# The up projection of a language adapter wholly in rounded parts, with new orders of a step

## The chip, the core and the metric

The program runs on one core of a Trainium2 chip. The metric is the device time of one execution in microseconds (us). TensorE (PE) multiplies matrices, VectorE (DVE), ScalarE (ACT) and GpSimd (POOL) work on elements, and SyncE (SP) issues DMAs. A queue that issues a DMA is written with a q (SPq, ACTq).

## What is computed

There are 32 samples of 512 tokens with 512 features, all in float32. Each sample has its own adapter (one of 10 languages) and its own linear layer (one of 32 categories):

```python
# per sample: w1 = W1[lang], w2 = W2[lang], ... , W = L1_W[cat]
h = relu(x @ w1 + b1)                     # 512x512 @ 512x128, the up projection
r = x + (h @ w2 + b2)                     # 512x128 @ 128x512, the down projection
normed = (r - mean) * rsqrt(var + 1e-5)
x1 = x + (normed * gamma + beta)
out = x1 + (x1 @ W + b)                   # 512x512 @ 512x512, the linear layer
```

## The kernel before, in words

**Precision.** A float32 factor is split into a rounded part `_hi` and the rest `_lo` (type fp32r), and a product is taken as three matmuls, hi x hi, lo x hi and hi x lo (`split_product`, L833 to L835). One float32 matmul does the same without any split, and PE spends more time on it. The identity is added to W ahead of the linear layer, so that x1 @ (W + 1) gives x1 + x1 @ W.

**Stages.** The kernel is written by hand for each engine, as a software pipeline with one `step(k)` per sample. In step k PE does the linear layer of sample k-2, the up and down projections of sample k, and the transposes of the normalised sample k-1. Its order is: linear tiles 0 and 1 (`linear_tile`, 12 matmuls each), `up(k)`, `turn_norm` 0 and 1, linear tile 2, `down(k)`, `turn_norm` 2 and 3, linear tile 3. A linear tile sums over four chunks c of the features. In tile 0 each chunk waits for its own part of the data: `w_lo` from POOL and `x1T_lo` from DVE (L902, L903). So tile 0 of step k+1 waits for what DVE's `low_x1` wrote in step k, chunk by chunk.

**Up projection.** It has four chunks too. Three (NS = 3) are done from rounded parts `xs_hi`, `xs_lo`, `w1_hi`, `w1_lo`, nine matmuls. The fourth is one float32 matmul (L876), which the trace records as two instructions. ACT makes the `_hi` parts of the next sample (`high_xs_of_next`, `high_w1_of_next`), POOL the `_lo` parts (`low_xs`, `low_w1`).

**The chain inside a step.** After `up(k)` ACT does `relu` (two instructions), and DVE takes the rest (`low_h`). PE runs `down(k)`. DVE adds the result to x (`y_pair`, L680) and takes the means, ACT squares each of four token tiles (`square`, L537) and takes a root (`deviation`, L542), and DVE finishes the inverse deviation in seven small instructions (`variance`, `inverse_deviation`, L699 to L716). ACT normalises in the next step (L501), PE transposes, DVE forms x1 (`x1`, L725), ACT rounds it (`high_x1`, L518) and DVE takes the rest (`low_x1`, L731). Both `x1` halves of a step (chunks 0 and 1, then 2 and 3) are for sample k-1.

**Buffers and queues.** Every engine runs its instructions in the order in which they are written. SP issues nearly all DMAs in one order per step; ACT issues two of the four `x_quad` loads, which DVE then transposes into `xT` (L666). `params` (gamma, beta, b1 of a language) and `b2_bc` have two buffers each. Stores leave by halves: `out_half0` holds tiles 0 and 1, `out_half1` tiles 2 and 3.

## Time and profile before

| what | value |
|---|---|
| median of 3 runs | 614.54 us (614.09 to 615.64) |
| the profiled execution's own time | 615.36 us |
| its span in the profile | 613.5 us |
| PE busy | 605.9 us, 99% of the span |
| DVE, ACT, POOL busy | 520.5 (85%), 514.2 (84%), 525.7 us (86%) |
| HBM traffic | 270 GB/s over the span |

The span runs from the first to the last instruction in the trace, and the execution's own time is 1.86 us longer. Busy is the sum of an engine's instruction times. A group of instructions also has a mean duration and the idle time of its engine ahead of it. The share of PE in the chain of work that ended last is 86%.

### The profile page before, as it was taken

The page shows a single profiled execution, that of the slowest core. Times are in us where ns is not written, and L with a number is a line of the kernel's source. Part 1 is how long each engine was busy: PE and PEld are TensorE (multiplying, and loading weights), DVE is VectorE, ACT ScalarE, POOL GpSimd, SP SyncE. Part 2 cuts the span into 40 slices and gives each one's busy share as a digit, 9 for nine tenths or more (in the row PEclk, how much of TensorE's full clock was granted, in tenths as well). Part 3 has the DMA queues.
Part 4 walks back from the last instruction along what each step waited for, and adds up shares of the span by engine and source line. Part 5 has one row for each costly group of instructions (what it writes and reads, how often), then busy time and mean ns, then how long its engine had stood idle before and what let it go on. Part 6 is the DMA issues. An engine that isn't in the chain of part 4 may idle for free.

```text
span 613.5 us, 10721 instructions
## 1 busy us (share of the span) xinstructions
PE 605.9 (99%) x2866; PEld 490.3 (80%) x2866; DVE 520.5 (85%) x1151; ACT 514.2 (84%) x772; POOL 525.7 (86%) x265
## 2 busy tenths in 40 slices
PE   9998999999999999999999999999999999999998
PEld 7766888778888888888888888778888888888887
DVE  1889889789898888988989899898898888899673
ACT  4978888789888899888889889889888989889770
POOL 5789998799989999888998889899888998989830
PEclk9999999999999999999999999999999999999999
DMA  9987899878998888899898997989999898997422
GB/s 305 236 273 247 299 317 286 268 257 264 309 301 272 285 284 274 300 289 301 252 303 255 311 295 257 296 265 289 309 289 291 261 296 263 314 308 269 160 87 104
DMA packets 125939, 166.24 MB, mean 271 GB/s; under 512 B 11062, under 2 KB 72768, under 8 KB 121812
## 3 DMA queue, kind: packets, MB, share of 16 engines
q1 hardware_dynamic: 94900, 150.12, 75.0%
q10 hardware_dynamic: 30912, 15.73, 9.2%
q8 instruction: 11, 0.18, 0.1%
q14 instruction: 20, 0.16, 0.1%
q0 software_dynamic: 96, 0.05, 0.0%
HBM read 132.17 MB, written 33.55 MB: 270 GB/s over the span
## 4 chain that ended last, share of the span: by engine, by line
PE 86%; DMA 4%; SPq 3%; DVE 3%; ACT 2%; issue 2%; POOL 0%; ACTq 0%; DVEq 0%; POOLq 0%
PE o_bank L833 17%; PE o_bank L835 17%; PE o_bank L834 17%; PE n_bank L851 8%; PE d_bank L833 5%; PE d_bank L835 5%; PE d_bank L834 5%; PE d_bank L876 4%; DMA x_quad<-in_x 2%; PE y_bank L833 2%; PE y_bank L835 2%; PE y_bank L834 2%; DMA x_tok<-in_x 2%; SPq L243 1%; DVE xT L666 1%
## 5 line engine op out<-in xcount | busy, mean ns | idle before, releaser
L833 PE MATMUL o_bank<-w_hi,x1T_hi 128*128 128x512 f32 x512 | 205.4, 401 | 1.8 <-DVE x1T_lo L731 1.8
L835 PE MATMUL o_bank<-w_hi,x1T_lo 128*128 128x512 f32 x512 | 200.0, 391 | 0.0
L834 PE MATMUL o_bank<-w_lo,x1T_hi 128*128 128x512 f32 x512 | 199.1, 389 | 0.0
L666 DVE STREAM_TRANSPOSE xT<-x_quad 128x512 f32<-128x512 f32 x120 | 127.2, 1102 | 38.7 <-DMA x_quad<-in_x 38.7
L428 POOL TENSOR_TENSOR w_lo<-w_raw,w_hi 128x1024 fp32r<-128x1024 f32 x62 | 149.3, 2408 | 10.5 <-ACT w_hi L511 10.4
L501 ACT ACTIVATE norm<-y,neg_mean_rstd,rstd 128x512 f32<-128x512 f32 x128 | 151.8, 1262 | 1.1 <-DVE neg_mean_rstd L716 1.1
L423 POOL TENSOR_TENSOR x_tok<-x_tok,b_bc 128x1024 f32<-128x1024 f32 x60 | 145.0, 2417 | 4.5 <-issue 2.6
L518 ACT ACTIVATE x1T_hi<-n_bank,params 128x512 fp32r<-128x512 f32 x126 | 85.2, 690 | 35.3 <-DVE n_bank L725 26.9
L833 PEld LDWEIGHTS o_bank<-w_hi,x1T_hi 128*128 128x128 f32 x512 | 96.3, 188 | 21.7 <-issue 3.8
L835 PEld LDWEIGHTS o_bank<-w_hi,x1T_lo 128*128 128x128 f32 x512 | 96.1, 188 | 21.0
L834 PEld LDWEIGHTS o_bank<-w_lo,x1T_hi 128*128 128x128 f32 x512 | 96.4, 188 | 17.8
L537 ACT ACTIVATE x_tok<-y,neg_mean 128x512 f32<-128x512 f32 x128 | 91.9, 719 | 17.7 <-DVE neg_mean L686 17.7
L394 POOL TENSOR_TENSOR xs_lo<-xT,xs_hi 128x1536 fp32r<-128x1536 f32 x29 | 102.3, 3527 | 0.0
L725 DVE SCALAR_TENSOR_TENSOR n_bank<-n_bank,params,xT 128x512 f32<-128x512 f32 x126 | 92.4, 757 | 7.1 <-PE n_bank L851 6.8
L731 DVE SCALAR_TENSOR_TENSOR x1T_lo<-n_bank,params,x1T_hi 128x512 fp32r<-128x512 f32 x126 | 91.1, 750 | 7.4 <-ACT x1T_hi L518 2.0
L743 DVE TENSOR_TENSOR out_half<-o_bank,b_bc 128x512 f32<-128x512 f32 x127 | 85.5, 673 | 12.4 <-PE o_bank L835 11.6
L511 ACT ACTIVATE w_hi<-w_raw 128x1024 fp32r<-128x1024 f32 x64 | 67.6, 1059 | 17.4 <-POOL w_raw L405 16.1
L382 POOL TENSOR_TENSOR w_lo<-w_raw,w_hi 128x512 fp32r<-128x512 f32 x31 | 40.4, 1304 | 44.1 <-ACT w_hi L486 42.0
L851 PEld LDWEIGHTS n_bank<-ident,norm 128*128 128x128 f32 x504 | 59.2, 145 | 9.4 <-ACT norm L501 2.4
L851 PE MATMUL n_bank<-ident,norm 128*128 128x128 f32 x504 | 65.9, 274 | 0.1
L405 POOL TENSOR_TENSOR w_raw<-w_raw,ident 128x512 f32<-128x512 f32 x32 | 50.4, 1575 | 0.0
L833 PE MATMUL d_bank<-xs_hi,w_hi 128*128 128x512 f32 x87 | 46.0, 529 | 0.0
(95 smaller groups left out, 818.0 us busy)
## 6 DMA issues: line engine op xcount, KB each, us to landing
w_raw<-in_L_cond_W SPq DMA_DIRECT2D x32, 1024.0 KB, 6.5
out<-out_half SPq DMA_DIRECT2D x63, 512.0 KB, 4.6
x_tok<-in_x SPq DMA_DIRECT2D x31, 1024.0 KB, 11.5
w_raw<-in_L_cond_W SPq DMA_DIRECT2D x64, 256.0 KB, 4.3
b_bc<-in_L_cond_b SPq DMA_DIRECT2D x64, 256.0 KB, 8.6
x_quad<-in_x SPq DMA_DIRECT2D x62, 256.0 KB, 3.7
x_quad<-in_x ACTq DMA_DIRECT2D x58, 256.0 KB, 10.7
x_tok<-in_x ACTq DMA_DIRECT2D x2, 256.0 KB, 3.3
```

The lines of the kernel that those rows point to most:

```text
L394: pool.tensor_tensor(xs_lo[:, :, :], xT[(k.x + 1) % 3][:, 0:NS, :], xs_hi[:, :, :].bitcast(F32), ALU.subtract).then_inc(xs_lo_done, 1)
L423: pool.tensor_tensor(pair, pair, b2_bc[p][:, :].rearrange("p (o h) -> p o h", o=1).to_broadcast([P, 2, H]), ALU.add).then_inc(x_b2_done, 2)
L428: pool.tensor_tensor(w_lo[q][:, c:c + 2, :], w_raw[q][:, c:c + 2, :], w_hi[q][:, c:c + 2, :].bitcast(F32), ALU.subtract).then_inc(w_lo_don ...
L501: act.activation(dst, src, ACT.Identity, scale=rstd[:, t:t + 1], bias=neg_mean_rstd[:, t:t + 1]).then_inc(norm_done, 1)
L537: act.activation(x_tok[k.b][:, t, :], y[:, t, :], ACT.Square, bias=neg_mean[:, t:t + 1], accum_out=sq_sum[:, t:t + 1]).then_inc(sq_done, 1)
L666: dve.transpose(xT[(k.x + 1) % 3][:, c, :].rearrange("p (b j) -> p b j", j=SQ), x_quad[1 - k.b][:, :, c::NC]).then_inc(xT_done, 1)
L725: dve.scalar_tensor_tensor(norm_bank(k, c)[:, :], norm_bank(k, c)[:, :], params[q][:, c:c + 1], xT[(k.x + 2) % 3][:, c, :], ALU.mult, ALU. ...
L731: dve.scalar_tensor_tensor(x1T_lo[q][:, c, :], norm_bank(k, c)[:, :], params[q][:, NC + c:NC + c + 1], x1T_hi[q][:, c, :].bitcast(F32), AL ...
L833: pe.matmul(acc, lhs_hi, rhs_hi, start=first, stop=False)
L834: pe.matmul(acc, lhs_hi, rhs_lo, start=False, stop=False)
L835: return pe.matmul(acc, lhs_lo, rhs_hi, start=False, stop=last)
L851: ins = pe.transpose(norm_bank(k, c)[:, t * P:(t + 1) * P], norm[:, t, c * P:(c + 1) * P] if by_chunk(k) else norm[:, t, c::NC], ident[:, :])
```

## The change

- NS becomes 4: all four chunks of the up projection come from rounded parts. The float32 matmul of steps 3 to 31 goes, three matmuls come, and the roundings of ACT and POOL grow from 1536 to 2048 and from 384 to 512 columns.
- ACT's order in a step is new (below), and its two `x_quad` loads move to SP.
- DVE does `variance` and `inverse_deviation` ahead of `low_x1` of chunks 2 and 3, where they stood at the end of the step.
- POOL does the first half of the b2 addition ahead of the identity, and `low_xs` ahead of `low_w1`.
- SP's order is new: `params` has three buffers and is loaded earlier, `b2_bc` has one and is loaded last in the step, after `x_b2_done`. The store of the second half of a sample is issued in the next step, behind the load of x.
- `zeros` lies in an output buffer.

The diff, cut to its core:

```diff
-    NS = 3
+    NS = 4
...
                     load_w(cat_w, p)
                 if loads:
-                    load_b2(lang, q)
                     load_x(k.sample(-1), q)
+                if linear and k.since(3):
+                    store(k, 3, 1)
                 if turn:
 
                     if k.since(2):
                         sp.wait_ge(out_done, k.count(NT, 2, OUT_CREDIT))
                     load_b(cat_b, q)
+                if loads:
+                    if k.since(2):
+                        sp.wait_ge(x1_lo_done, k.count(NC, 1, 0))
+                    load_params(lang, (k.x + 1) % 3)
                 if linear:
                     store(k, 2, 0)
                 if loads:
-                    sp.wait_ge(x1_lo_done, k.count(NC, 0, 0))
-                    load_params(lang, q)
-                if linear:
-                    store(k, 2, 1)
+                    sp.wait_ge(x_b2_done, k.count(NT, 0, NT))
+                    load_b2(lang, q)
...
+                    if adapter and not k.last(2):
+                        plus_b2_pair(0)
                     if turn:
                         plus_identity()
-                    if adapter:
+                    if adapter and k.last(2):
                         plus_b2_pair(0)
-                    if turn:
-                        low_w_pair(0)
                     if adapter:
                         plus_b2_pair(2)
                     if turn:
+                        low_w_pair(0)
                         low_w_pair(2)
                 if follow:
                     low_w2(q, k.count(1, -1, 1))
                     if k.since(2):
+                        low_xs(k)
                         low_w1(k)
-                        low_xs(k)
...
-                if k.last(2):
-                    for t in range(NT):
-                        normalise(k, t)
-                    high_w(k, 0)
-                else:
-                    high_w(k, 0)
-                    for t in range(NT):
-                        normalise(k, t)
+                for t in range(NT - 1):
+                    normalise(k, t)
+                high_w(k, 0)
+                normalise(k, NT - 1)
                 high_w(k, 2)
+                if follow:
+                    high_w2_of_next(k)
                 if adapter:
                     relu(k)
-                if follow and not k.last(S - 2):
-                    load_next_x_quads(k)
+                if follow and not k.last(2):
+                    high_xs_of_next(k)
+                    high_w1_of_next(k)
                 high_x1(k, 0)
                 high_x1(k, 1)
-                if follow:
-                    high_w2_of_next(k)
+                if k.last(2):
+                    high_xs_of_next(k)
                     high_w1_of_next(k)
-                    high_xs_of_next(k)
                 if adapter:
-                    square(k, 0)
-                    square(k, 1)
-                    square(k, 2)
+                    for t in range(NT):
+                        square(k, t)
+                    deviation(k)
                 high_x1(k, 2)
                 high_x1(k, 3)
-                if adapter:
-                    square(k, 3)
-                    deviation(k)
...
                 x1(k, 2)
                 x1(k, 3)
+                if adapter:
+                    variance(k)
+                    inverse_deviation(k)
                 low_x1(k, 2)
                 low_x1(k, 3)
                 output(k, 3)
-                if adapter:
-                    variance(k)
-                    inverse_deviation(k)
...
                 acc = up_bank(k)[:, :]
-                pe.wait_ge(w1_in[k.b], 16 * k.pairs(0) + 16)
                 pe.wait_ge(y_done, k.count(NT, 0, 0))
-                for c in range(NS, NC):
-                    pe.wait_ge(xT_done, k.count(NC, 0, c + 1))
-                    pe.matmul(acc, w1_raw[k.b][:, c, :], xT[k.x][:, c, :], start=c == NS, stop=False)
```

On ACT, before, one step between `relu` and the root. The rows L528 and L531 are `relu`, L518 is `high_x1`, L537 a square, L542 the root; the numbers behind the names are buffers.

```order
L528 ACTIVATE d_bank0<-d_bank0,params0 128x512
L531 ACTIVATE hT_hi<-d_bank0 128x512
...
L518 ACTIVATE x1T_hi1<-n_bank0,params1 128x512
L518 ACTIVATE x1T_hi1<-n_bank1,params1 128x512
L486 ACTIVATE w2_hi1<-w2_raw1 128x512
L548 ACTIVATE w1_hi<-w1_raw1 128x384
...
L553 ACTIVATE xs_hi<-xT2 128x1536
...
L537 ACTIVATE x_tok0,sq_sum<-y,neg_mean 128x512
```

And the same stretch of a step of the changed kernel, down to the next step's first instructions (L541, L544 are `relu`, L531 is `high_x1`, L550 a square, L555 the root, L514 the normalisation).

```order
L541 ACTIVATE d_bank0<-d_bank0,params0 128x512
L544 ACTIVATE hT_hi<-d_bank0 128x512
...
L566 ACTIVATE xs_hi<-xT1 128x2048
L561 ACTIVATE w1_hi<-w1_raw1 128x512
L531 ACTIVATE x1T_hi1<-n_bank0,params2 128x512
L531 ACTIVATE x1T_hi1<-n_bank1,params2 128x512
...
L550 ACTIVATE x_tok0,sq_sum<-y,neg_mean 128x512 x2
L555 ACTIVATE std<-sq_sum,eps 128x4
L531 ACTIVATE x1T_hi1<-n_bank0,params2 128x512
L531 ACTIVATE x1T_hi1<-n_bank1,params2 128x512
L514 ACTIVATE norm<-y,neg_mean_rstd,rstd 128x512 x3
```

The roundings of xs and w1 moved ahead of `high_x1` of chunks 0 and 1, and all squares and the root moved ahead of `high_x1` of chunks 2 and 3. Before, three squares stood ahead of these two, and the fourth square and the root behind them.

On DVE, the end of a step before: `x1` and `low_x1` of chunks 2 and 3, the last output tile, and the inverse deviation.

```order
L725 SCALAR_TENSOR_TENSOR n_bank0<-n_bank0,params0,xT1 128x512
L725 SCALAR_TENSOR_TENSOR n_bank1<-n_bank1,params0,xT1 128x512
L731 SCALAR_TENSOR_TENSOR x1T_lo0<-n_bank0,params0,x1T_hi0 128x512
L731 SCALAR_TENSOR_TENSOR x1T_lo0<-n_bank1,params0,x1T_hi0 128x512
L743 TENSOR_TENSOR out_half1<-o_bank1,b_bc1 128x512
L699 TENSOR_SCALAR d_bank1<-y_sum 128x4
L701 TENSOR_SCALAR d_bank1<-sq_sum 128x4
L707 RECIPROCAL r0<-std 128x4
L709 SCALAR_TENSOR_TENSOR d_bank1<-r0,d_bank1 128x4
L711 TENSOR_TENSOR d_bank1<-d_bank1,r0 128x4
L713 SCALAR_TENSOR_TENSOR rstd<-d_bank1,r0 128x4
L716 TENSOR_TENSOR neg_mean_rstd<-d_bank1,rstd 128x4
```

The end of a step after, with L721 for `x1`, L727 for `low_x1` and L739 for the output tile.

```order
L721 SCALAR_TENSOR_TENSOR n_bank0<-n_bank0,params0,xT0 128x512
L721 SCALAR_TENSOR_TENSOR n_bank1<-n_bank1,params0,xT0 128x512
L695 TENSOR_SCALAR d_bank1<-y_sum 128x4
L697 TENSOR_SCALAR d_bank1<-sq_sum 128x4
L703 RECIPROCAL r0<-std 128x4
L705 SCALAR_TENSOR_TENSOR d_bank1<-r0,d_bank1 128x4
L707 TENSOR_TENSOR d_bank1<-d_bank1,r0 128x4
L709 SCALAR_TENSOR_TENSOR rstd<-d_bank1,r0 128x4
L712 TENSOR_TENSOR neg_mean_rstd<-d_bank1,rstd 128x4
L727 SCALAR_TENSOR_TENSOR x1T_lo0<-n_bank0,params0,x1T_hi0 128x512
L727 SCALAR_TENSOR_TENSOR x1T_lo0<-n_bank1,params0,x1T_hi0 128x512
L739 TENSOR_TENSOR out_half1<-o_bank1,b_bc1 128x512
```

The seven small instructions, of which the third waits for ACT's root, now stand ahead of the two `low_x1`.

## Rows read from the trace of the kernel before

**Rows 1.** Busy time by engine (PE, PEld, DVE, ACT, POOL), clock, DMA share, GB/s, 28 steps.

```profile
59.79:576.94 517.15, 516.42 (x2439) 419.17 (x2439) 455.51 (x1005) 455.73 (x673) 469.99 (x225) 1.00 0.88 284
```

**Rows 2.** Waits of PE: us in total, times, longest.

```profile
PE o_bank L833 <- DVE x1T_lo L731: 1.8, 1, 1.8
```

**Rows 3.** Chain of work: start, us, what; L851 follows the up projection's end.

```profile
318.84 0.88 PE n_bank L851 x8
...
334.31 0.86 PE d_bank L876 x2
335.16 0.23 PE d_bank L833
...
337.24 0.87 PE n_bank L851 x8
```

**Rows 4.** Timeline (start, us, engine, line, out<-in, count): first and last float32 matmul.

```profile
56.70 1.02 PE L876 MATMUL d_bank<-xT,w_raw 128*128 128x512 f32 x2
...
573.84 1.02 PE L876 MATMUL d_bank<-xT,w_raw 128*128 128x512 f32 x2
```

**Rows 5.** Timeline of ACT in the step after 318.84.

```profile
319.57 0.60 ACT L531 ACTIVATE hT_hi<-d_bank 128x512 fp32r<-128x512 f32 x1
...
322.94 0.62 ACT L486 ACTIVATE w_hi<-w_raw 128x512 fp32r<-128x512 f32 x1
...
323.88 1.48 ACT L553 ACTIVATE xs_hi<-xT 128x1536 fp32r<-128x1536 f32 x1
325.81 0.72 ACT L537 ACTIVATE x_tok<-y,neg_mean 128x512 f32<-128x512 f32 x1 [0.45 <-DVE neg_mean L686]
...
328.05 1.35 ACT L518 ACTIVATE x1T_hi<-n_bank,params 128x512 fp32r<-128x512 f32 x2
329.29 0.71 ACT L537 ACTIVATE x_tok<-y,neg_mean 128x512 f32<-128x512 f32 x1
...
330.13 0.30 ACT L542 ACTIVATE std<-sq_sum,eps 128x4 f32<-128x4 f32 x1
...
332.00 4.94 ACT L501 ACTIVATE norm<-y,neg_mean_rstd,rstd 128x512 f32<-128x512 f32 x4
336.85 1.04 ACT L511 ACTIVATE w_hi<-w_raw 128x1024 fp32r<-128x1024 f32 x1
337.80 0.62 ACT L528 ACTIVATE d_bank<-d_bank,params 128x512 f32<-128x512 f32 x1
```

**Rows 6.** Timeline of DVE in the same step.

```profile
322.19 1.64 DVE L731 SCALAR_TENSOR_TENSOR x1T_lo<-n_bank,params,x1T_hi 128x512 fp32r<-128x512 f32 x2
...
324.34 0.68 DVE L680 SCALAR_TENSOR_TENSOR y<-d_bank,x_tok 128x512 f32<-128x512 f32 x1
...
328.77 1.41 DVE L731 SCALAR_TENSOR_TENSOR x1T_lo<-n_bank,params,x1T_hi 128x512 fp32r<-128x512 f32 x2
...
330.82 0.17 DVE L707 RECIPROCAL r<-std 128x4 f32<-128x4 f32 x1
...
331.63 0.16 DVE L716 TENSOR_TENSOR neg_mean_rstd<-d_bank,rstd 128x4 f32<-128x4 f32 x1
```

**Rows 7.** Timeline of PE: first matmul of chunk 3 of linear tile 0.

```profile
330.74 0.39 PE L833 MATMUL o_bank<-w_hi,x1T_hi 128*128 128x512 f32 x1
```

**Rows 8.** Timeline at the one long wait of PE, on DVE and PE.

```profile
51.59 1.41 DVE L731 SCALAR_TENSOR_TENSOR x1T_lo<-n_bank,params,x1T_hi 128x512 fp32r<-128x512 f32 x2
...
52.49 0.47 PE L833 MATMUL o_bank<-w_hi,x1T_hi 128*128 128x512 f32 x1 [1.83 <-DVE x1T_lo L731]
```

**Rows 9.** Busy time, clock, DMA share and GB/s around that wait, columns as in rows 1.

```profile
50.00:60.00 10.00, 8.17 (x35) 5.86 (x35) 9.57 (x20) 9.59 (x15) 10.00 (x5) 1.00 0.66 205
```

**Rows 10.** Groups of instructions on POOL: busy us, mean ns of one | idle before.

```profile
L428 POOL TENSOR_TENSOR w_lo<-w_raw,w_hi 128x1024 fp32r<-128x1024 f32 x62 | 149.3, 2408 | 10.5 <-ACT w_hi L511 10.4
L394 POOL TENSOR_TENSOR xs_lo<-xT,xs_hi 128x1536 fp32r<-128x1536 f32 x29 | 102.3, 3527 | 0.0
```

**Rows 11.** DMA issues: times, KB each, median us from issue to landing.

```profile
out<-out_half SPq DMA_DIRECT2D x63, 512.0 KB, 4.6
```

More of the change, by code:

```diff
@@ L22, in pairs, with thirds @@
         return ROUND // 2 * self.h + (self.p - back) // 2
+    def thirds(self, back):
+        return ROUND // 3 * self.h + (self.p - back) // 3
     def count(self, per, back, more):
@@ L97, in adapter_then_conditional_linear @@
         w_raw = [sb(f"w_raw{i}", [P, NC, H]) for i in range(2)]
-        b2_bc = [sb(f"b2_bc{i}", [P, H]) for i in range(2)]
+        b2_bc = sb("b2_bc", [P, H])
         b_bc = [sb(f"b_bc{i}", [P, H]) for i in range(2)]
-        params = [sb(f"params{i}", [P, NP]) for i in range(2)]
+        params = [sb(f"params{i}", [P, NP]) for i in range(3)]
         x_quad = [sb(f"x_quad{i}", [P, NB, NC * SQ]) for i in range(2)]
@@ L136, in adapter_then_conditional_linear @@
         param_rows = norm[0:L, :, :]
+        zeros = out_half[1][:, 1, 0:P]
         param_table = sb("param_table", [P, L, NP])
@@ L145, in adapter_then_conditional_linear, with b2_of @@
         neg_mean_copy, var_eps, newton, newton2 = (d_bank[1][:, n * NT:(n + 1) * NT] for n in range(4))
+        def b2_of(k):
+            return b_bc[1] if k.since(1) and not k.since(2) else b2_bc
         def first_xT_bank(c):
@@ L184, in adapter_then_conditional_linear @@
         b2_in = [sem(f"b2_in{i}") for i in range(2)]
-        params_in = [sem(f"params_in{i}") for i in range(2)]
+        params_in = [sem(f"params_in{i}") for i in range(3)]
         w_in = [sem(f"w_in{i}") for i in range(2)]
@@ L239, in sample_id, with load_x_quads @@
                 return sp.value_load(ids[0:1, which, bass.ds(s, 1)], min_val=0, max_val=count - 1)
-            def load_x_quads(s, p, quads=(0, 1)):
-                for n in quads:
+            def load_x_quads(s, p):
+                for n in range(NQ):
                     sp.dma_start(x_quad[p][quad(n), :, :],
@@ L257, in load_w2, with load_b2 @@
                              ).then_inc(w2_in[p], 16)
[L259 to L260 removed]
+            def load_b2(lang, p, dst=b2_bc):
+                sp.dma_start(dst[:, :], b2[bass.ds(lang, 1)].to_broadcast([P, H])
                              ).then_inc(b2_in[p], 16)
@@ L331, in _ @@
             lang1 = sample_id(0, 1, L)
-            load_b2(lang1, 1)
+            load_b2(lang1, 1, b_bc[1])
             load_w1(lang1, 1)
@@ L338, in _ @@
                          ).then_inc(first_b1_in[1], 16)
-            load_x_quads(2, 0, range(NQ))
+            load_x_quads(2, 0)
             sp.wait_ge(table_done, 1)
@@ L357, in _ @@
             last = Step(S // ROUND, 3)
+            store(last, 3, 1)
             store(last, 2, 0)
@@ L414, in plus_b2 @@
                             pool.wait_ge(first_xT_turned, k.count(NC, 0, NC))
-                    pool.tensor_tensor(x_tok[p][:, t, :], x_tok[p][:, t, :], b2_bc[p][:, :],
+                    pool.tensor_tensor(x_tok[p][:, t, :], x_tok[p][:, t, :], b2_of(k)[:, :],
                                        ALU.add).then_inc(x_b2_done, 1)
@@ L422, in plus_b2_pair @@
                     pair = x_tok[p][:, t:t + 2, :]
-                    pool.tensor_tensor(pair, pair, b2_bc[p][:, :].rearrange("p (o h) -> p o h", o=1
+                    pool.tensor_tensor(pair, pair, b2_of(k)[:, :].rearrange("p (o h) -> p o h", o=1
                                        ).to_broadcast([P, 2, H]), ALU.add).then_inc(x_b2_done, 2)
@@ L515, in high_x1 @@
                 if c == 0:
-                    act.wait_ge(params_in[q], 16 * k.pairs(1) + 16)
+                    act.wait_ge(params_in[(k.x + 2) % 3], 16 * k.thirds(1) + 16)
                 act.wait_ge(x1_done, k.count(NC, 1, c + 1))
                 act.activation(x1T_hi[q][:, c, :], norm_bank(k, c)[:, :], ACT.Identity,
-                               bias=params[q][:, NC + c:NC + c + 1]).then_inc(x1_hi_done, 1)
+                               bias=params[(k.x + 2) % 3][:, NC + c:NC + c + 1]).then_inc(x1_hi_done, 1)
             def relu(k):
@@ L528, in relu @@
                 act.activation(up_bank(k)[:, :], up_bank(k)[:, :], ACT.Relu,
-                               bias=params[k.b][:, 2 * NC:NP]).then_inc(relu_done, 1)
+                               bias=params[k.x][:, 2 * NC:NP]).then_inc(relu_done, 1)
                 act.wait_ge(relu_done, k.count(1, 0, 1))
@@ L722, in x1 @@
                 if c == 0:
-                    dve.wait_ge(params_in[q], 16 * k.pairs(1) + 16)
+                    dve.wait_ge(params_in[(k.x + 2) % 3], 16 * k.thirds(1) + 16)
                 dve.wait_ge(nT_done, k.count(NC, 1, c + 1))
-                dve.scalar_tensor_tensor(norm_bank(k, c)[:, :], norm_bank(k, c)[:, :], params[q][:, c:c + 1],
+                dve.scalar_tensor_tensor(norm_bank(k, c)[:, :], norm_bank(k, c)[:, :], params[(k.x + 2) % 3][:, c:c + 1],
                                          xT[(k.x + 2) % 3][:, c, :], ALU.mult, ALU.add).then_inc(x1_done, 1)
@@ L731, in low_x1 @@
                 dve.scalar_tensor_tensor(x1T_lo[q][:, c, :], norm_bank(k, c)[:, :],
-                                         params[q][:, NC + c:NC + c + 1], x1T_hi[q][:, c, :].bitcast(F32),
+                                         params[(k.x + 2) % 3][:, NC + c:NC + c + 1], x1T_hi[q][:, c, :].bitcast(F32),
                                          ALU.add, ALU.subtract).then_inc(x1_lo_done, 1)
@@ L840, in keep_clock @@
                 for _ in range(count):
-                    pe.matmul(idle_bank[:, 0:P], zeros[:, :], zeros[:, :], start=True, stop=True)
+                    pe.matmul(idle_bank[:, 0:P], zeros, zeros, start=True, stop=True)
             def turn_norm(k, c):
```

18 lines of the change are left out of this document (3 added, 15 removed).

## The prediction

> **What bounds the kernel now.** I read the busy times first. Over 28 steps, 517.15 us from the end of one up projection to the end of another, PE is busy for 516.42 us at a granted clock of 1.00 (2.4 GHz), while DVE, ACT and POOL are busy for 455.51, 455.73 and 469.99 us [rows 1]. Then come the waits: in the whole run PE waits once for `low_x1`, 1.8 us [rows 2]. So PE sets the time, and a step takes (573.84 - 56.70) / 28 = 18.47 us between the first and the last of the 29 float32 matmuls [rows 4]; the step that I take apart takes 337.24 - 318.84 = 18.40 [rows 3]. Last I read the timelines of ACT and DVE in that step [rows 5, 6], since the change reorders them. I count from the end of the up projection at 318.84 as 0. The reader is to see there how late `x1T_lo` of chunks 2 and 3 is, because the next linear tile 0 needs it, and that is the narrowest place: DVE finishes the pair at 328.77 + 1.41 = 330.18 [rows 6], and PE starts chunk 3 at 330.74 [rows 7]. A hand-over from DVE to PE costs about 0.15 us: at the one long wait the first of a pair ended at 51.59 + 0.75 = 52.34 (half of the pair's 1.41 and a little overlap), and the matmul started at 52.49 [rows 8]. The slack is therefore 330.74 - 330.18 - 0.15 = 0.41 us.
>
> **PE's work.** The float32 matmul takes 0.86 us on the chain, a matmul from rounded parts 0.23 [rows 3]. Three of them take 0.69. That saves 0.17 us in each of 29 steps, 4.9 us, if PE still waits for nothing. A step of pure PE work would be 18.40 - 0.17 = 18.23.
>
> **The roundings.** POOL takes 3.53 us for 1536 columns and 2.41 for 1024 [rows 10], so 512 more cost 1.12 and 128 more 0.28. Its work grows from 469.99 / 28 = 16.79 to 18.19 us per step. That fits under 18.23 by a hair, and under any longer step easily. ACT takes 0.62 us for 512 columns and 1.48 for 1536 [rows 5], 0.84 ns per column, so `xs_hi` of 2048 takes 1.91 and `w1_hi` of 512 takes 0.62. ACT's work grows by 0.43 + 0.11 from 16.28 us; by itself that is hidden.
> For the larger `xs_lo` the Trainium skill has a price of its own (GPSIMD Engine Reference, section 3.1 Elementwise): 4.50 us for a `tensor_tensor` of 2048 float32 columns, where the rows give 3.53 + 1.12 = 4.65. With it POOL's step would be 18.04; no run so far shows that size.
>
> **The new orders, as one chain.** What matters is when `low_x1` of chunk 3 is done. In the new order, with neighbours on ACT starting some 0.09 before the one ahead ends (336.85 + 1.04 against 337.80) [rows 5]:
> `hT_hi` ends at 319.57 + 0.60 - 318.84 = 1.33. `xs_hi` starts at 1.24 and ends at 3.15, `w1_hi` runs from 3.06 to 3.68, and `high_x1` 0 and 1 take 1.35 as a pair, from 3.59 to 4.94 [rows 5]. Before, these two stood ahead of the roundings; now they stand behind them. `low_x1` of chunk 1 takes 0.75 more, to 5.72. From the end of that pair to the first y took 324.34 - (322.19 + 1.64) = 0.51 [rows 6], so y starts at 6.23. Before it was at 324.34 - 318.84 = 5.50, so this reordering costs 0.73.
> The first square follows y by 325.81 - 324.34 = 1.47. Three squares take 328.05 - 325.81 = 2.24, and the fourth to the root 330.13 - 329.29 = 0.84, so the root starts at 6.23 + 1.47 + 2.24 + 0.84 = 10.78 and ends at 11.08 [rows 5, 6]. DVE then needs from the reciprocal to the end of L716 331.63 + 0.16 - 330.82 = 0.97 [rows 6]. With 0.05 for the hand-over, which is my estimate from the 0.02 to 0.15 of the others, that is 12.10. Only now, at 12.05 with the overlap, does `low_x1` of chunk 2 start (before: 328.77 - 318.84 = 9.93), and the pair ends at 13.46. DVE has nothing else to do for it in between, since it waits for the root.
> PE can start chunk 3 at 13.46 + 0.15 = 13.61. In the trace it started at 330.74 - 318.84 = 11.90. So PE comes 1.71 us later, and since that matmul is followed only by PE work up to the end of the next up projection, **a step takes 18.40 - 0.17 + 1.71 = 19.94 us**. It repeats: the next chain again starts at that end, so no buffer takes the delay up.
> ACT alone gives nearly the same ring. `high_x1` 2 and 3 run from 11.08 to 12.43, four normalisations take 336.85 - 332.00 = 4.85, two roundings of W 0.95 each and that of w2 0.53, so the next `relu` could start at 19.6 [rows 5]. ACT then stands idle from 4.94 to 7.70, waiting for y. Taking only one of the two orders back would thus not give all of the time back.
>
> **Moves that I cost at nothing.** The loads of x_quad, params, w1, w2 and x come earlier or stay; two DMA issues leave ACT. DMA was busy for 0.88 of the time at 284 GB/s [rows 1], and a longer step asks less of it. Cover for b2, now one row loaded after the last use, is the POOL work between, `low_w`, `low_w2`, `low_xs` and `low_w1`, over 11 us. The store of the second half now stands behind some 2.5 MB of w1, w2, W and x, some 9 us at 284 GB/s, and then takes 4.6 us [rows 11]; DVE needs that buffer again some 15 us or more after the loads are issued. Without that cover y would start late, and every us of it would be a us of the step.
>
> **The sum.** 28 steps from 18.47 to 19.94: + 41.2 us. Step 2, where PE already waits, and step 31, which has no roundings of a next sample, have the DVE and square part of the delay only: y to `low_x1` 2 goes from 328.77 - 324.34 = 4.43 to 12.05 - 6.23 = 5.82, + 1.4, and + 1.4 - 0.4 of slack. That is 2.4 together. Start-up and end are otherwise left as they are. The profiled execution goes from 615.36 to 659.0, and the median from 614.54 to **658.1 us**.
>
> **Rivals.**
> - **Only PE's work counts** (faster). If `x1T_lo` came within the old slack, the step would be 18.23 to 18.3, with POOL's 18.19 just under it: 614.54 - 4.9 = 609.6, up to 612 with POOL in the way. It needs `low_x1` 3 done by 11.75 instead of 13.46. The 99% of PE speak for it; the order of DVE, where `low_x1` stands behind an instruction that waits for the fourth square, speaks against it. I would have to be wrong by 1.7 us in a sum of measured pieces.
> - **Only the inverse deviation delays.** If the 0.73 of the roundings is made up (DVE gets to y as early as before), the delay is 1.39 - 0.41 = 0.98 and the step 19.2: 614.54 + 28 x 0.74 + 2.4 = 638. DVE's waits for x_quad are gone, which speaks for it, but it waits for ACT there.
> - **The late store.** Were it to land 1 us after DVE wants the buffer, y would start 1 us later, and the step would be 20.9: 686. The old order stored with an empty queue ahead; there are some 2 us to spare by the count above.
> - **The clock.** Each step would now have one PE wait of some 1.7 us. Around the 1.83 us wait in the trace the granted clock stayed at 1.00 [rows 8, 9]. Were it to fall to 1.2 GHz for one linear tile after each wait (12 matmuls of 0.23, doubled), a step would get 2.7 us longer: 658 + 76 = 734. [...]
>
> **Chances.** The forecast 0.70, only the inverse deviation 0.10, faster 0.08, the late store 0.07, the clock 0.03, and 0.02 for no change. A difference within 0.3% is about what a measurement of this kernel can't tell from none. So faster 0.08, same 0.02, slower 0.90. The pieces of the chain are known to 0.1 or 0.2 us each; 0.3 us per step either way is 8 us, which makes 649 to 668 the forecast's own range. With the second rival below and part of the third above it is 636 to 674.
>
> **What would show it.** PE waits for L727 (`low_x1`) in some 30 steps, 1.7 us each, some 50 us in all, and PE's share falls to about 92%. The float32 matmuls are gone and the up projection takes 2.76 us. ACT waits 2.8 us per step for the means ahead of the first square. DVE waits for the root (L703) and no longer for x_quad. y starts 6.2 us after the up projection's end, and L727 of chunk 2 12.05 after it. A step is 19.9 us. I am wrong if PE has no waits, if they lie at L833 of the down or up projection, or if DVE's output tile waits for a DMA.

## The result

| what | before | changed kernel |
|---|---|---|
| median | 614.56 us of 4 runs (614.09 to 615.64) | 666.96 us of 4 runs (665.51 to 667.5) |
| the profiled execution | 615.36 us, span 613.5 | 667.09 us, span 665.3 |
| end of the up projection of step 3 to that of step 31 | 517.15 us | 560.80 us |

The ratio is 1.0843, 95% interval 1.0817 to 1.0869. The forecast was 658.1 us, with 636 to 674 as its range. Of the 51.8 us in the span, 560.80 - 517.15 = 43.65 lie in the 28 steps, 67.44 - 59.79 = 7.65 ahead of them, and 0.5 behind. In the timeline of before, the transposes that mark this end start at 59.68 and not at 59.79; 67.44 is read from a timeline too, so like against like these two are 7.8 and 0.3.

The window over those steps, columns as in [rows 1]:

```profile
67.44:628.24 560.80, 519.43 (x2466) 422.58 (x2465) 457.78 (x1004) 461.82 (x673) 510.89 (x226) 1.00 0.89 259
```

PE was idle for 0.73 us of this window before and is idle for 41.4 now. POOL's work has grown by 40.90 us, 1.46 per step. The page's group for the larger rounding (busy us, mean ns of one | idle time ahead):

```profile
L406 POOL TENSOR_TENSOR xs_lo<-xT,xs_hi 128x2048 fp32r<-128x2048 f32 x29 | 134.1, 4624 | 14.6 <-ACT xs_hi L566 14.6
```

Waits in the whole run (engine, line, what it waited for, us in total, times, longest), the answer to [rows 2]:

```profile
ACT x_tok L550 <- DVE neg_mean L682: 82.8, 31, 2.8
...
PE o_bank L829 <- DVE x1T_lo L727: 42.6, 29, 2.2
...
PE d_bank L829 <- DVE hT_lo L667: 7.1, 2, 5.5
```

One wait of 1.8 us before has become 29 of 1.2 to 2.2 us. Now one step, timeline of ACT, DVE and PE. It begins with the transposes right behind the up projection (L847 at 328.99). The forecast took its 0 from the chain of work, which puts a start of PE behind others 0.16 us later than the timeline (318.84 against 318.68 before). So its 0 is 329.15 here.

```profile
329.88 0.60 ACT L544 ACTIVATE hT_hi<-d_bank 128x512 fp32r<-128x512 f32 x1
330.38 1.91 ACT L566 ACTIVATE xs_hi<-xT 128x2048 fp32r<-128x2048 f32 x1
...
332.70 1.26 ACT L531 ACTIVATE x1T_hi<-n_bank,params 128x512 fp32r<-128x512 f32 x2
336.80 0.73 ACT L550 ACTIVATE x_tok<-y,neg_mean 128x512 f32<-128x512 f32 x1 [2.83 <-DVE neg_mean L682]
...
339.86 0.30 ACT L555 ACTIVATE std<-sq_sum,eps 128x4 f32<-128x4 f32 x1
```

```profile
335.34 0.68 DVE L676 SCALAR_TENSOR_TENSOR y<-d_bank,x_tok 128x512 f32<-128x512 f32 x1
...
340.19 0.18 DVE L703 RECIPROCAL r<-std 128x4 f32<-128x4 f32 x1 [0.16 <-ACT std L555]
...
341.08 1.40 DVE L727 SCALAR_TENSOR_TENSOR x1T_lo<-n_bank,params,x1T_hi 128x512 fp32r<-128x512 f32 x2
```

```profile
328.99 1.03 PE L847 MATMUL n_bank<-ident,norm 128*128 128x128 f32 x8
...
341.97 0.47 PE L829 MATMUL o_bank<-w_hi,x1T_hi 128*128 128x512 f32 x1 [1.44 <-DVE x1T_lo L727]
...
342.74 0.40 PE L829 MATMUL o_bank<-w_hi,x1T_hi 128*128 128x512 f32 x1
...
348.94 1.03 PE L847 MATMUL n_bank<-ident,norm 128*128 128x128 f32 x8
```

Counted from 329.15, the y is at 6.19 (forecast 6.23, before 5.50), the root at 10.71 (10.78), `low_x1` of chunk 2 at 11.93 (12.05) and PE's chunk 3, at 342.74, at 13.59 (13.61). From mark to mark the step takes 348.94 - 328.99 = 19.95 (19.94). The matmul that waits, at 341.97, is not the first of chunk 3 but the first of chunk 2: six matmuls of linear tile 0 stand ahead of it, and it starts 0.14 us behind the first instruction of the `low_x1` pair (341.08 + about 0.75). Over the 28 steps the first, from 67.44 to 89.65, takes 22.21 us (I call it step 3), and the other 27 take 19.95 on average.

Step 2 went otherwise than forecast. Timelines of SP's queue, ACT and PE there, then the windows around it:

```profile
37.57 1.94 SPq L251 DMA_DIRECT2D x_quad<-in_x  x4
...
40.46 0.38 SPq L264 DMA_DIRECT2D w_raw<-in_L_cond_W  x1
```

```profile
46.35 0.63 ACT L499 ACTIVATE w_hi<-w_raw 128x512 fp32r<-128x512 f32 x1 [5.99 <-DMA w_raw<-in_L_cond_W]
```

```profile
48.93 0.79 PE L829 MATMUL d_bank<-w_hi,hT_hi 128*128 128x512 f32 x1 [5.47 <-DVE hT_lo L667]
```

```profile
40.00:50.00 10.00, 4.53 (x21) 3.49 (x21) 3.29 (x6) 3.13 (x6) 8.39 (x5) 0.84 1.09 310
50.00:60.00 10.00, 9.23 (x37) 7.27 (x35) 9.06 (x27) 7.16 (x15) 4.94 (x2) 0.81 0.87 241
```

The same load and rounding in the kernel before:

```profile
38.18 0.38 SPq L256 DMA_DIRECT2D w_raw<-in_L_cond_W  x1
```

```profile
43.80 0.62 ACT L486 ACTIVATE w_hi<-w_raw 128x512 fp32r<-128x512 f32 x1
```

ACT rounds w2 ahead of `relu` now. In step 2 that w2 (L264) is issued at 40.46, behind four loads of x_quad, where it was issued at 38.18. It is wanted at 46.35 - 5.99 = 40.36, where it was used at 43.80. So `relu` and with it the down projection stand behind a DMA for 6 us. Then eleven matmuls run 0.43 us apart and not 0.23; the granted clock of these windows is 0.84 and 0.81.

Not all of the 7.8 us comes from here. Step 2, from the end of its up projection to that of step 3, takes 67.44 - 39.59 = 27.85 us where it took 59.68 - 37.62 = 22.06. The other 2.0 us have gathered before it. DVE's first transpose of x_quad waits for the load, 2.01 us where it waited 0.49, and PE waits behind it:

```profile
22.96 1.09 DVE L662 STREAM_TRANSPOSE xT<-x_quad 128x512 f32<-128x512 f32 x1 [2.01 <-DMA x_quad<-in_x]
```

### The profile page after: what moved, and what is told of

It reads as the page before. It is cut to its first block, busy times and chain, and to the rows that moved or that the text cites. A ratio compares the mean times of both kernels' runs of the same rounds, so it can differ in the third digit from the quotient of the medians.

```text
span 665.3 us, 10751 instructions
## 1 busy us (share of the span) xinstructions
PE 610.7 (92%) x2895; PEld 495.6 (74%) x2895; DVE 522.3 (79%) x1151; ACT 520.5 (78%) x772; POOL 565.5 (85%) x265
## 4 chain that ended last, share of the span: by engine, by line
PE 36%; ACT 20%; DVE 18%; issue 18%; SPq 4%; DMA 3%; POOL 1%; ACTq 0%; DVEq 0%
PE o_bank L829 8%; ACT x_tok L550 8%; PE o_bank L831 7%; PE o_bank L830 7%; DVE x1T_lo L727 6%; DVE y L676 5%; PE d_bank L829 4%; PE d_bank L831 4%; PE d_bank L830 4%; ACT d_bank L541 3%; DVE out_half L739 3%; ACT w_hi L561 3%; ACT x1T_hi L531 2%; DMA b_bc<-in_L_cond_b 2%; ACT xs_hi L566 2%
## 5 line engine op out<-in xcount | busy, mean ns | idle before, releaser
L829 PE MATMUL o_bank<-w_hi,x1T_hi 128*128 128x512 f32 x512 | 208.9, 408 | 42.6 <-DVE x1T_lo L727 42.6
L440 POOL TENSOR_TENSOR w_lo<-w_raw,w_hi 128x1024 fp32r<-128x1024 f32 x62 | 147.7, 2406 | 52.4 <-ACT w_hi L524 52.4
L514 ACT ACTIVATE norm<-y,neg_mean_rstd,rstd 128x512 f32<-128x512 f32 x128 | 155.6, 1267 | 1.1 <-DVE neg_mean_rstd L712 1.1
L550 ACT ACTIVATE x_tok<-y,neg_mean 128x512 f32<-128x512 f32 x128 | 91.5, 717 | 82.8 <-DVE neg_mean L682 82.8
L406 POOL TENSOR_TENSOR xs_lo<-xT,xs_hi 128x2048 fp32r<-128x2048 f32 x29 | 134.1, 4624 | 14.6 <-ACT xs_hi L566 14.6
L721 DVE SCALAR_TENSOR_TENSOR n_bank<-n_bank,params,xT 128x512 f32<-128x512 f32 x126 | 91.8, 753 | 42.5 <-PE n_bank L847 42.5
L727 DVE SCALAR_TENSOR_TENSOR x1T_lo<-n_bank,params,x1T_hi 128x512 fp32r<-128x512 f32 x126 | 88.7, 744 | 43.8 <-ACT x1T_hi L531 43.5
L739 DVE TENSOR_TENSOR out_half<-o_bank,b_bc 128x512 f32<-128x512 f32 x127 | 85.2, 671 | 11.8 <-PE o_bank L831 11.5
L531 ACT ACTIVATE x1T_hi<-n_bank,params 128x512 fp32r<-128x512 f32 x126 | 79.3, 679 | 6.5 <-DVE n_bank L721 6.5
L847 PEld LDWEIGHTS n_bank<-ident,norm 128*128 128x128 f32 x504 | 59.6, 145 | 8.4 <-ACT norm L514 0.5
L847 PE MATMUL n_bank<-ident,norm 128*128 128x128 f32 x504 | 65.6, 273 | 0.0
L566 ACT ACTIVATE xs_hi<-xT 128x2048 fp32r<-128x2048 f32 x29 | 55.4, 1911 | 2.8 <-DVE xT L662 2.8
L417 POOL TENSOR_TENSOR w_raw<-w_raw,ident 128x512 f32<-128x512 f32 x32 | 49.4, 1543 | 0.0
```

Of the source, the lines that this page charges most:

```text
L406: pool.tensor_tensor(xs_lo[:, :, :], xT[(k.x + 1) % 3][:, 0:NS, :], xs_hi[:, :, :].bitcast(F32), ALU.subtract).then_inc(xs_lo_done, 1)
L440: pool.tensor_tensor(w_lo[q][:, c:c + 2, :], w_raw[q][:, c:c + 2, :], w_hi[q][:, c:c + 2, :].bitcast(F32), ALU.subtract).then_inc(w_lo_don ...
L514: act.activation(dst, src, ACT.Identity, scale=rstd[:, t:t + 1], bias=neg_mean_rstd[:, t:t + 1]).then_inc(norm_done, 1)
L550: act.activation(x_tok[k.b][:, t, :], y[:, t, :], ACT.Square, bias=neg_mean[:, t:t + 1], accum_out=sq_sum[:, t:t + 1]).then_inc(sq_done, 1)
L727: dve.scalar_tensor_tensor(x1T_lo[q][:, c, :], norm_bank(k, c)[:, :], params[(k.x + 2) % 3][:, NC + c:NC + c + 1], x1T_hi[q][:, c, :].bitc ...
L739: dve.tensor_tensor(out_half[t // 2][:, t % 2, :], o_bank[t % 2][:, :], b_bc[k.b][:, :], ALU.add).then_inc(out_done, 1)
```

## Experiments

All of them are edits of the changed kernel. A step is the mean over the same 28 steps, from up projection to up projection. Numbers 1, 3, 5, 6 and 7 are one execution each, so their times are less sure than the others. In start-up above all one execution differs from another: number 2 and the changed kernel have the same code up to the end of the up projection of step 3, and reach it at 69.41 and 67.44. No run takes SP's order or the buffers back, and none has the fourth rounded chunk with all else as before.

**1. Rounding w2 behind `relu` in step 2.** Is the start-up loss this wait?

```diff
-                if follow:
+                if follow and not k.last(2):
                     high_w2_of_next(k)
                 if adapter:
                     relu(k)
+                if k.last(2):
+                    high_w2_of_next(k)
```

> The changed kernel with one instruction moved in step 2 alone: the rounding of w2 stands behind relu there, as it did before; all other steps are as changed. Theory 'start-up': in step 2 ACT waits 5.99 us for the load of w2 ahead of relu, so PE waits 5.5 us for the rest of h and comes back at a lower clock; this is what the forecast missed. Expected: that wait goes, the end of the up projection of step 3 comes some 6 us earlier, the steps stay at 20.03 us, and the time goes from 667 to 660 or 661. Rival 'the start-up is late because of the order of the DMAs': the wait only moves to the next user of a late load, and the time stays at 665 to 667.

Measured: 663.7 us, 3.3 less than the median of the changed kernel (whose fastest run took 665.51), where 660 or 661 was expected. PE's wait of 5.47 us at the down projection of step 2 is gone. But ACT still waits for the same load, now ahead of `high_x1`, and PE waits at the next transposes, and then 2.9 us for `low_x1`:

```profile
ACT w_hi L499 <- DMA w_raw<-in_L_cond_W: 4.8, 1, 4.8
...
PE n_bank L849 <- DVE x1T_lo L729: 2.1, 1, 2.1
```

So the wait mostly moved on. The up projection of step 3 ends at 66.58, 0.9 us earlier and not 6; the other 2.3 us are gained in step 3, which takes 19.89 and not 22.21, since no long wait and no fall of the clock come there. The place on ACT alone is a small part of the start-up loss.

**2. The roundings of xs and w1 behind `high_x1` 0 and 1.** The first of the two reorderings taken back, in the steps after the second.

```diff
-                if follow and not k.last(2):
-                    high_xs_of_next(k)
-                    high_w1_of_next(k)
                 high_x1(k, 0)
                 high_x1(k, 1)
-                if k.last(2):
+                if follow:
                     high_xs_of_next(k)
                     high_w1_of_next(k)
```

> The changed kernel with the roundings of xs and w1 on ACT behind high_x1 of chunks 0 and 1 in every step, where they stood before; squares, inverse deviation and all else as changed. Theory 'chain': y starts some 1.4 us earlier (at about 4.75 us behind the end of the up projection instead of 6.2), so low_x1 of chunk 3 does too, and a step takes 18.5 us instead of 20.03: 28 x 1.5 less, 667 to about 625. Rival 'only the inverse deviation and the squares delay': y is held by something else and the step stays at 19.5 or more, 650 or more. Rival 'ACT ring': ACT is then bound at 18.2 to 18.5, which gives the same time but with little wait of PE.

Measured: 636.15 us (635.6 to 637.93), ratio to before 1.0348 (1.0286 to 1.0410), step 18.84, where 18.5 and 625 were expected. Leaving step 3 out of both, a step goes from 19.95 to 18.82, so this place alone was 1.13 us of it, more than the 0.73 that the forecast gave it:

```profile
ACT w_hi L524 <- POOL w_raw L417: 25.0, 29, 1.5
ACT x_tok L550 <- DVE neg_mean L679: 18.9, 31, 2.8
...
PE o_bank L826 <- DVE x1T_lo L724: 11.1, 27, 1.2
```

The y now starts at 319.79 - 314.57 = 5.22 after the up projection's end, 1.13 earlier:

```profile
319.79 0.68 DVE L673 SCALAR_TENSOR_TENSOR y<-d_bank,x_tok 128x512 f32<-128x512 f32 x1
```

ACT's idle time ahead of the squares falls from 82.8 to 18.9 us: it rounds while DVE makes y. What is late next is ACT's rounding of W, for POOL's identity (L417).

**3. The inverse deviation back at the end of DVE's step.** The second reordering alone, ACT's order as changed.

```diff
                 x1(k, 3)
-                if adapter:
-                    variance(k)
-                    inverse_deviation(k)
                 low_x1(k, 2)
                 low_x1(k, 3)
                 output(k, 3)
+                if adapter:
+                    variance(k)
+                    inverse_deviation(k)
```

> The changed kernel with variance and inverse deviation at the end of DVE's step again, ACT as changed. Rival 'only the inverse deviation' says that this gives back about 1 us per step: 639. My theory of two rings says the contrary: low_x1 of chunk 2 still waits for high_x1 behind the root (at 11.65 instead of 11.93), while the inverse deviation is done at about 14.7 instead of 12, and ACT has four normalisations, two roundings of W, one of w2 and then relu behind it, 7.3 us: relu at about 22.0. Expected a step of 21.5 to 22 us, in which PE waits at down or up and not at linear tile 0: 667 + 28 x 1.7, about 710 to 722.

Measured: 722.36 us, step 21.85, at the slow end of what was expected. PE's waits lie at linear tile 0 and at the transposes, not at down or up:

```profile
DVE x1T_lo L727 <- ACT x1T_hi L531: 77.0, 60, 1.5
ACT norm L514 <- DVE neg_mean_rstd L712: 76.5, 31, 2.6
...
PE o_bank L829 <- DVE x1T_lo L727: 54.1, 29, 2.0
...
PE n_bank L847 <- ACT norm L514: 19.7, 20, 1.7
```

PE's wait for `low_x1` does not shrink, it grows from 42.6 us to 54.1. In ACT's new order `high_x1` 2 and 3 stand behind the root, so `low_x1` can't start before them, wherever DVE has its small instructions. And ACT, which has nothing left after `high_x1` 3, needs them for the norms. So given ACT's order, DVE's is the better one; no run takes ACT's place of `high_x1` 2 and 3 back alone. In 11 of the 28 steps the clock also falls. These take 22.3 us, the ones right behind them 21.4 and the rest 21.8, so the mean hardly depends on it.

**4. All orders of ACT and DVE back.** POOL's order, SP's order, the buffers and the fourth rounded chunk stay. I took ACT and DVE for the whole cause.

```diff
-                for t in range(NT - 1):
-                    normalise(k, t)
-                high_w(k, 0)
-                normalise(k, NT - 1)
...
+                    high_w(k, 0)
+                    for t in range(NT):
+                        normalise(k, t)
...
                 if follow:
                     high_w2_of_next(k)
+                    high_w1_of_next(k)
+                    high_xs_of_next(k)
                 if adapter:
...
-                    for t in range(NT):
-                        square(k, t)
-                    deviation(k)
+                    square(k, 0)
+                    square(k, 1)
+                    square(k, 2)
                 high_x1(k, 2)
                 high_x1(k, 3)
+                if adapter:
+                    square(k, 3)
+                    deviation(k)
```

The norms stand behind the first rounding of W again, in one row of four; `relu` and `high_x1` 0 and 1 stand ahead of the roundings of w2, w1 and xs; and DVE's order is that of number 3.

> The changed kernel with all of ACT's and DVE's order as before, and all else as changed: four chunks from rounded parts, POOL's and SP's new orders, three buffers of params, one b2 row. Theory 'orders': the whole loss is from the two orders; a step takes PE's 18.23 us or, where ACT with 0.54 us more work is late with relu, up to 18.5, and start-up is as before: 609 to 616. Rival 'roundings, loads or POOL': the larger roundings or the loads cost, and the time stays above 625.

Measured: 747.25 us (745.92 to 748.27), ratio 1.2137 (1.2066 to 1.2208), step 22.85. The theory fell, in the direction of its rival. The rows of ACT and POOL in a step:

```profile
301.96 1.90 ACT L566 ACTIVATE xs_hi<-xT 128x2048 fp32r<-128x2048 f32 x1
...
313.75 1.06 ACT L524 ACTIVATE w_hi<-w_raw 128x1024 fp32r<-128x1024 f32 x1 [5.35 <-POOL w_raw L417]
314.71 4.86 ACT L514 ACTIVATE norm<-y,neg_mean_rstd,rstd 128x512 f32<-128x512 f32 x4
```

```profile
303.94 4.63 POOL L406 TENSOR_TENSOR xs_lo<-xT,xs_hi 128x2048 fp32r<-128x2048 f32 x1 [1.02 <-ACT xs_hi L566]
308.52 1.31 POOL L400 TENSOR_TENSOR w_lo<-w_raw,w_hi 128x512 fp32r<-128x512 f32 x1
309.79 2.41 POOL L435 TENSOR_TENSOR x_tok<-x_tok,b_bc 128x1024 f32<-128x1024 f32 x1
312.16 1.55 POOL L417 TENSOR_TENSOR w_raw<-w_raw,ident 128x512 f32<-128x512 f32 x1
```

A ring runs through both engines: `xs_hi` on ACT, then `xs_lo`, `w1_lo`, b2 and identity on POOL, then W's rounding on ACT, and behind that in ACT's old order all four norms, on which PE waits (99.6 us in 29 waits). It closes on ACT: the second rounding of W, `relu`, `high_x1` 0 and 1 and the roundings of w2 and w1 stand between the norms and the next `xs_hi` at 324.73. With the norms ahead of W's rounding, as in the changed kernel, they no longer wait for POOL. That this is the useful part of the new order is my reading; no run moves the norms alone.

**5. POOL's order back too.** Now all three engines run in the orders of before, with NS = 4.

```diff
-                    if adapter and not k.last(2):
-                        plus_b2_pair(0)
                     if turn:
                         plus_identity()
-                    if adapter and k.last(2):
+                    if adapter:
                         plus_b2_pair(0)
+                    if turn:
+                        low_w_pair(0)
                     if adapter:
                         plus_b2_pair(2)
                     if turn:
-                        low_w_pair(0)
                         low_w_pair(2)
...
-                        low_xs(k)
                         low_w1(k)
+                        low_xs(k)
```

> Four chunks from rounded parts with the orders of ACT, DVE and POOL as in the kernel before; only SP's order and the buffers stay as changed. This is the NS = 4 part nearly alone. Theory 'ring of POOL and ACT', formed from the run before this one, in which the order of ACT and DVE alone was put back: xs_hi (1.9 us) - xs_lo (4.6) - identity (1.5) on POOL - rounding of W (1.0), four normalisations (4.85), rounding of W (0.95), relu (1.2), high_x1 and the roundings of w2 and w1 (about 3.7) on ACT - next xs_hi. With 1536 columns this ring took about 18.1 us, under PE's 18.4; with 2048 it takes 19.6 to 19.9. Expected: a step of 19.7 us, PE waiting for the normalisation or relu, 648 to 656. Rival 'orders are all': then this kernel is PE bound at 18.23 and takes 609 to 612. Rival of my forecast's wording, that the orders alone lost the time, is the same number.

Measured: 649.07 us, step 19.59, as the ring theory expected (648 to 656). POOL's order alone, all that differs from number 4, was 3.26 us of a step. The ring is shorter and still there, and a store is late:

```profile
ACT w_hi L523 <- POOL w_raw L417: 38.5, 26, 2.4
PE n_bank L849 <- ACT norm L513: 23.5, 26, 2.0
...
DVE out_half L741 <- DMA out<-out_half: 19.0, 19, 3.3
```

So with the orders of before on three engines, the fourth rounded chunk takes a longer step than the kernel before; it needs another order, and the one that came with it was partly wrong.

This pair also says more on start-up. Step 2 takes 28.21 us in number 4 and 22.29 here, against 27.85 in the changed kernel and 22.06 before, though w2 is issued behind the four x_quad loads here too (at 39.98). What moved is POOL's identity for step 3, at 60.85 there, behind half of b2, and at 53.84 here:

```profile
60.85 1.54 POOL L417 TENSOR_TENSOR w_raw<-w_raw,ident 128x512 f32<-128x512 f32 x1
```

```profile
53.84 1.54 POOL L417 TENSOR_TENSOR w_raw<-w_raw,ident 128x512 f32<-128x512 f32 x1
```

**6. Identity ahead of b2 on POOL**, added to number 2.

```diff
-                    if adapter and not k.last(2):
-                        plus_b2_pair(0)
                     if turn:
                         plus_identity()
-                    if adapter and k.last(2):
+                    if adapter:
                         plus_b2_pair(0)
```

> The kernel with the roundings of xs and w1 behind high_x1 (step 18.8 us, 636), and in addition POOL's identity ahead of both halves of the b2 addition. Theory 'ring of POOL and ACT': the 0.9 us per step that ACT waits for the identity there goes, and what is left is the chain to low_x1 of chunk 3: a step of 18.5 us, 636 - 28 x 0.3, about 628. Rival 'the chain alone holds that kernel': nothing changes, 636.

Measured: 629.43 us, step 18.63, near the 628 and 18.5 that were expected. ACT's wait for the identity is gone, and PE waits for `low_x1` 7 times, 4.1 us in all.

**7. Rounding w2 behind `relu` in all steps, and in step 2 the loads of w1 and w2 ahead of x_quad**, added to number 6.

```diff
-                if follow:
-                    high_w2_of_next(k)
                 if adapter:
                     relu(k)
+                if follow:
+                    high_w2_of_next(k)
...
+                if loads and k.last(2):
+                    sp.wait_ge(sq_done, k.count(NT, 0, 0))
+                    load_w1(lang, q)
+                    load_w2(lang, q)
                 if quads:
                     sp.wait_ge(xT_done, k.count(NC, 0, NC))
                     load_x_quads(k.sample(-2), p)
-                if loads:
+                if loads and not k.last(2):
```

> As the one with the identity first, and in addition the rounding of w2 behind relu in every step, and in step 2 the loads of w1 and w2 ahead of those of x_quad. Theory: the late w2 of step 2, which cost 6 to 7 us in the changed kernel, comes at once, and in later steps nothing gets worse since ACT waits for x1 there anyway: about 621. Rival: the load is as late behind others, 628.

Measured: 625.0 us, between the 621 of the theory and the 628 of the rival. Step 3 now starts at 60.38, 8.5 us earlier than in number 6, and then takes 24.04 us. Timelines of DVE and PE in it:

```profile
68.79 0.69 DVE L737 TENSOR_TENSOR out_half<-o_bank,b_bc 128x512 f32<-128x512 f32 x1 [4.03 <-DMA out<-out_half]
```

```profile
75.95 0.77 PE L827 MATMUL o_bank<-w_hi,x1T_hi 128*128 128x512 f32 x1 [4.04 <-DVE x1T_lo L725]
```

That is the rival of the late store, in one step: DVE stands at output tile 2, y stands behind it, and every us arrives at PE.

**8. Output tile 2 on DVE behind the two y pairs**, added to number 7, so that neither the store nor PE's tile 2 holds up y.

```diff
-                output(k, 2)
                 if adapter:
                     y_pair(k, 0)
                     y_pair(k, 1)
+                output(k, 2)
```

> As e11_start, and in addition output tile 2 on DVE behind both pairs of y. Theory: y then starts when the down projection is done, at 4.45 us instead of 4.75 behind the end of the up projection, low_x1 of chunk 3 ends at 11.65 and PE no longer waits: a step of 18.23 to 18.35, 609 to 617, at or below the kernel before. Rival: POOL with its 18.19 us of work, or ACT, holds the step at 18.5 or more, 618 to 622.

Measured: 614.45 us (612.5 to 616.83, 10 runs), ratio 0.9985 (0.9964 to 1.0005), step 18.33, the shortest so far. Below 18.47 per step, but the window over the 28 steps opens at 63.91 and not at 59.68. The waits of PE are in start-up, and the clock falls there:

```profile
24.67 0.50 PE L827 MATMUL d_bank<-w_hi,hT_hi 128*128 128x512 f32 x1 [1.87 <-DVE hT_lo L665]
...
55.34 0.47 PE L827 MATMUL o_bank<-w_hi,x1T_hi 128*128 128x512 f32 x1 [2.29 <-DVE x1T_lo L725]
```

```profile
20.00:30.00 10.00, 8.13 (x42) 6.63 (x41) 6.24 (x18) 7.49 (x12) 6.08 (x6) 0.83 1.18 226
...
50.00:60.00 10.00, 7.71 (x26) 5.54 (x25) 9.18 (x21) 9.97 (x17) 10.00 (x5) 0.83 1.13 272
```

**9. Start-up nearly as before.** Step 2 of number 8 nearly in the orders of before on ACT, DVE and POOL (the rounding of w2 stays right behind `relu`, and the early loads stay), and `low_h` of the second sample ahead of the first transpose of x_quad, which waits for a DMA.

```diff
-            turn_next_x(k1, 0)
             low_h(k1)
+            turn_next_x(k1, 0)
             turn_next_x(k1, 1)
```

> The kernel of e10_output_behind, with step 2 in the orders of the kernel before on ACT, DVE and POOL, and in start-up the rounded part of the second sample's hidden layer (low_h) ahead of the first transpose of x_quad instead of behind it. Theory: the steady step of e10 (18.32 us against 18.47) is worth about 4 us over 28 steps, and e10 gives just that back before the loop, where its third up projection ends at 63.9 us against 59.6, after PE waits of 1.9, 0.7 and 2.3 us with granted clock 0.83 behind them. With those waits gone: 610 to 611 us. Rival: the step after the start takes the delay up again, or the clock falls at another of PE's early waits, and the time stays at 613 to 615.

Measured: 612.57 us (611.48 to 615.27, 12 runs) against 615.85 of before in the same runs, ratio 0.9952 (0.9933 to 0.9971), where 610 to 611 was expected and 613 to 615 by the rival. Its span is 610.5 us, 3.0 less than before: 3.8 gained in the 28 steps (517.15 against 513.35), less 0.7 in start-up (60.39 against 59.68).

```profile
60.39:573.74 513.35, 513.16 (x2464) 421.96 (x2465) 457.07 (x1004) 468.36 (x673) 509.53 (x226) 1.00 1.00 285
```

PE's waits for `low_x1` are down to 1.8 us in all. This kernel beats both, the one before by half a percent. It is bound by PE (513.16 of 513.35 us), with POOL at 509.53 right below. The rival "only PE's work counts" gave 609.6 to 612 as the best that the fourth rounded chunk can do; the kernel that comes near it is this one.

## Why the prediction was right, and where it was off

- **The bound and the critical place: right.** PE's only frequent new wait is for `low_x1`, in linear tile 0 as the forecast said. But it waits at chunk 2, and the forecast had it wait at chunk 3 for the whole pair. Chunk 3 then follows behind chunk 2's three matmuls.
- **The chain: right.** Each of its pieces was met within 0.13 us, the largest miss being `low_x1` of chunk 2, which begins that much early. By its own rows chunk 2 could start at 12.05 + 0.75 + 0.15 = 12.95, 1.73 later than before (330.06 - 318.84 = 11.22), and its first matmul is slower behind a wait; that gives a step of 20.0, so that the earlier `low_x1` and the wrong chunk nearly cancel; the hundredth of a us between forecast and step is luck, the tenth is not. The 27 steps after step 3 take (560.80 - 22.21) / 27 = 19.95 us against the forecast's 19.94. PE's share is 92%, ACT's wait for the means 2.8 us, DVE's for x_quad 2.0 us in all, as foretold. PE's waits sum to 42.6 us and not to some 50, 1.45 each and not 1.7: the record counts a wait from the recorded end of the matmul ahead, which lasts 0.39 us though the next can start after 0.23. So 1.44 on record are 1.60 lost.
- **The term that was mis-sized is start-up.** The sum gave 2.4 us to steps 2 and 31 and left the rest "otherwise" as it was. Measured are 7.8 us ahead of the window, 22.21 - 19.95 = 2.3 in step 3 (a wait of 2.25 and not 1.45 us, and 1.5 for slower matmuls behind it) and 0.3 at the end, 10.4 in all. That is 8 of the 8.9 us between 658.1 and 666.96. The forecast gave the loads and w2's rounding nothing, which holds where data lie ready. Ahead of step 3 they don't: w2 is wanted before it lands, and the first x_quad comes late. But the late w2 is not the whole of it. Taking its rounding back in place gives 0.9 us before step 3 (experiment 1), and experiments 4 and 5 differ in step 2 by 5.9 us with POOL's order alone. How the 5.8 us that step 2 lost divide between ACT's place, SP's issue and POOL's order is not shown, nor what the 2.0 us ahead of it come from.
- **The roundings: right.** `xs_hi` takes 1.91 us as forecast, `xs_lo` 4.62 where the rows gave 4.65. POOL's step is 510.89 / 28 = 18.25 against 18.19. The 4.50 us of the Trainium skill (GPSIMD Engine Reference, section 3.1 Elementwise) are 0.12 below what this trace shows.
- **The shares of the two reorderings: wrong.** The forecast gave 0.73 to the roundings' place and 0.98 to the inverse deviation's, and the rival without the first had a step of 19.2. Experiment 2 gave 18.84, with y 1.13 us earlier than in the changed kernel and not 0.73. So the forecast's total held, its split did not. And by experiment 3 the delay put down to DVE's order belongs to ACT's, which has `high_x1` 2 and 3 behind the root. That one order alone would not give all of the time back holds (1.13 of some 1.5 in experiment 2, a further loss in 3), but not for the reason given, an ACT ring of 19.6. Nor has the second reordering a price of its own: experiment 8 keeps it on ACT and DVE and has a step of 18.33. It used up the slack of the chain, so that a late y cost time.
- **What the forecast did not see** is the ring between ACT and POOL (experiments 2, 4, 5). In the 28 steps of the changed kernel it held nothing up: ACT waits for the identity once, 1.5 us, in start-up. As "only PE's work counts" was treated, POOL's busy time of 18.19 was the only price of POOL; where its work stands in a ring, its order costs over 3 us of a step (22.85 in experiment 4, 19.59 in 5).
- **The late store** did not come in the changed kernel, and came in experiments 5 and 7. **The clock** stayed at 1.00 in every step of the changed kernel but step 3, so this rival was rightly given little here. It came in the start-up, and in experiments 3 and 4, where PE waits longer, it came again and again.

## What to carry to other kernels

Cost a move of an instruction not only in the steady step but in the first step that does it too, where the load that it reads was only just issued. When an engine's order is changed, write down the ring through all engines that feed each other, since an order that looks worse may be what cuts a ring, and take parts of a set of orders back one by one and together: here the version with the better places of each part beat both kernels, and the one with ACT's and DVE's orders simply taken back was the slowest of all.
